# The query convolution of image 1 on TensorE, and a reordered lead-in, in a fused two-layer vision block

## The chip, the cores and the metric

The program runs on one core of one Trainium2 chip. The metric is the device time of one execution, in microseconds (us). Engines: TensorE (PE), VectorE (DVE), ScalarE (ACT), GpSimd (POOL), and SyncE (SP), whose queue issues most DMAs. Each engine runs its own list of instructions in order; semaphores make one engine wait for another. A change of 0.3% (4.8 us) is about what can be told from none.

## The reference, cut to what matters

The input is x, 4 images of 96 channels and 56 x 56 pixels, in f32. Two layers follow, each a token mixer and a mixture-of-experts FFN with a norm before each:

```
x = x + attention(norm_channels(x))        # layer 0
t = tokens(x);  t = t + moe(norm(t))       # 4 experts, top 2, 96 -> 384 -> 96, exact gelu
x = x + convs(norm_channels(x))            # layer 1: 7x7, 5x3, 3x5, separable 7 and 5
t = tokens(x);  t = t + moe(norm(t))

attention(x):                               # all convolutions depthwise 3x3
    value, query = dwconv(x, w_v), dwconv(x, w_q)             # stride 1
    key, off     = dwconv(x, w_k, 2), dwconv(x, w_off1, 2)    # stride 2, 28 x 28
    offset = gelu(layernorm(off)) @ w_off2
    grid   = tanh(offset + ref)                               # 784 sample points
    v      = bilinear samples of value at grid
    out    = (query^T key * scale) v  =  query^T (key v^T) * scale   # per head of 32 channels
    return w_out @ out
```

## The kernel before, in words

**Tiling.** A norm or FFN tile is 448 pixels (8 rows of the image), 7 tiles per image. For the attention an image is laid out as quarters: partition 4c+q holds channel c of a group of 32 channels and quarter q of the image, so there are 3 groups g of 128 partitions, each with 784 pixels of a quarter. A depthwise 3x3 tap is then one multiply by a number per partition.

**Order of work.** All engines walk the same list of steps, `STEPS`: a lead-in of 15 steps (slot -1, `LEAD = 15`), then 8 slots of 7 steps. A slot is the FFN of one image in one layer, a step one tile of it, and each step has 12 chunks `c` (4 experts x 3 blocks of 128 hidden units). In a chunk of an FFN step PE does the three products of `first` (L1206 to L1208, hi and lo parts of the weights and tokens), ACT the gelu (L1004), PE the product of `second` one chunk later (L1199), and DVE combines the experts (L1506). The lead-in has the same 12 chunks per step, but no FFN: it only prepares image 0 and 1 for slot 0. The order is written out by hand, in tables that say at which step and chunk which piece is issued.

**Norm tiles (jobs).** `START_JOBS` says which tile is normalized in which step of the lead-in: "a0" to "a2" are attention norms of image 0 to 2, "f0" the FFN norm of image 0. A step has a job at place 0 and one at place 1. A job is: PE turns the tile to tokens (L1151), DVE takes the statistics (L1478, L1482, L1489) and subtracts the mean (L1490), POOL takes the power -1/2 (L1049), ACT scales (`apply`, L869), PE turns it back (L1161), ACT moves it out (`move`, L888/L889), SP stores it to DRAM in `norm_a` (L628). A job of place 1 is turned back and moved in the next step. In the lead-in `apply` is at chunks 3 and 8, at chunk 8 for both jobs of step 7.

**Convolutions of attention.** `ON_PE` names which of them PE does (`tap_conv`, L1268): image 0's off, query (first half of the rows), key, query (second half), and image 1's off and key. Each is 9 products per group of channels, one per tap, added up in one PSUM bank (L1287). Each product is against a 128 x 128 block that holds the tap's weights on its diagonal. A query half is 392 columns for each product, a key or off 196. ACT takes each result out of the bank with the bias (`take_conv`, L902). There are two banks (`h_ps`), so a convolution waits until the one before the last has been taken. All other 3x3 convolutions run on DVE (`attn_taps`, `taps3`, L1547 for the first tap, L1550 for the other 8, 3 groups): value for each image, and in image 1 query too, spread over FFN steps 0, 1 and 2 of slot 0 (`Q_ROUNDS`).

**The diagonal blocks.** The off blocks are made by POOL in 7 operations (`DIAG_POOL`, L1056) at the end of lead steps 2 and 3, in the buffers gate_t, pair and hidden; the 27 query blocks by POOL in 3 operations at the end of lead step 4, in `res_mem`; the 27 key blocks by ACT in three sets of 9 (`make_key_diag`, L893), in step 5 at chunks 2, 5 and 8. `res_mem` later holds the residual of the image, so no query blocks are left for image 1.

**Taps.** 19 small DMAs bring the weights of all convolutions (9 for attention and `to_quarters` and 4 of layer 1 on ACT's queue ahead of any of its work, 6 on SP's). At the end of lead step 1 PE spreads them over the partitions (L1402), and ACT copies them to `all_w` (L1029). At the end of step 3 PE spreads w_out and then waits until DVE has made `w_exp` of it (L1441).

**Stages.** The attention of image 0 runs in stages 0 to 6 in lead steps 5 to 11, that of image 1 in stages 0 to 2 in lead steps 12 to 14 and stages 4 to 6 in FFN steps 0 to 2. Value is done in stages 0 and 1; in stage 2 PE turns its 7 blocks (L1217, chunks 3 to 9), ACT takes them (L914), SP stores them (`store_values`, L725) so that POOL can gather from them; DVE norms off, ACT does gelu (L936) and tanh (L940), DVE the positions (L1659 to L1674). POOL gathers the samples of 2 x 8 blocks (`gather`, L1076), and DVE weighs them (`sample_row`, L1696 to L1703). In stage 6 PE forms key v^T and its product with w_out (L1246, L1252) and multiplies the query with it in 8 pieces (`times_query`, L1264), which DVE adds to the residual (L1609).

**POOL's list** in lead steps 7 and 8: at the end of step 7 gathers 0 to 7 of image 0; in step 8 the power of the first job, gathers 8 to 15, the power of the second job. **SP's list** in stage 2: three value blocks' stores, the store of the step's first norm tile, then the other four blocks' stores.

**Between the lead-in and the FFN.** In lead step 14 DVE reads the first scores of the gates (L1718), ACT does their exp (L944, behind its table load), DVE ranks them (L1729 to L1753), PE turns them (L1321) at chunk 9 and goes on with scores at chunk 10. Before FFN step 0 PE waits until all the attention's convolutions have been taken (`cv_free`).

Of the kernel before, what the change touches and what calls it, by code (L numbers as in the profile page):

```python
# [20 lines left out]
E, HID = 4, 384  # L21
# [61 lines left out]
ON_PE = {0: ("off", "query", "key", "query"), 1: ("off", "key")}  # L83
# [65 lines left out]
def metaformer_kernel(nc, a, out):  # L149

    with ExitStack() as ctx:
# [165 lines left out]
        def in_blocks(*mems):  # L317
# [111 lines left out]
        A_PARTS = [("value",), ("value", "query")] + [("value", "off", "key", "query")] * (NB - 2)  # L429
# [10 lines left out]
        DIAG_RUNS = {"off": 7, "query": 10}  # L440
# [20 lines left out]
        QUERY_CONV = {(0, 9): (0, 0), (0, 10): (0, 1), (1, 3): (0, 2), (3, 2): (1, 0), (3, 8): (1, 1), (4, 2): (1, 2)}  # L461
        QUERY_TAKE = {(0, 11): (0, 0), (1, 2): (0, 1), (1, 5): (0, 2), (3, 8): (1, 0), (3, 11): (1, 1), (4, 5): (1, 2)}
# [1479 lines left out]
```

## Time and profile before

| | us |
|---|---|
| median of 3 runs | 1609.62 (1609.45 to 1614.06) |
| profiled execution: its own time | 1611.21 |
| span of the profile | 1609.4 |
| PE busy | 1431.7 (89%) |
| DVE busy | 1143.8 (71%) |
| ACT busy | 719.2 (45%) |
| POOL busy | 504.0 (31%) |
| mean granted clock of PE, of its full speed | 0.953 |

The profile is of one execution. An engine counts as busy while an instruction of its is running; the shares are averages over stages with different limits, so they do not say what sets the end. The first 223 us of the span are the lead-in, the next 92 us the first three FFN steps, in which the attention of image 1 runs too. An f32 product of PE leaves two records, so 9 products are 18 records.

### The profile page before, as it was taken

How to read it: one execution, taken by the hardware profiler on the slowest of the kernel's cores; microseconds unless marked ns; L12 is line 12 of the kernel's file. 1: busy time of each engine (PE TensorE's matmuls, PEld its weight loads, DVE VectorE, ACT ScalarE, POOL GpSimd, SP SyncE). 2: the span in 40 equal slices, each digit the busy share in tenths (PEclk: the TensorE clock that was granted, in tenths of full speed). 3: DMA queues.
4: the chain of work that ended last, by engine and by line, in shares of the span. 5: the costliest groups of instructions: out<-in, count | busy, mean ns of one | idle time of the engine just before them, and what ended most of it. 6: DMA issues, size and time to landing. Idle time of an engine off the chain costs nothing.

```text
span 1609.4 us, 21517 instructions
## 1 busy us (share of the span) xinstructions
PE 1431.7 (89%) x6736; PEld 1060.9 (66%) x6736; DVE 1143.8 (71%) x2881; ACT 719.2 (45%) x1481; POOL 504.0 (31%) x536
## 2 busy tenths in 40 slices
PE   5876758998869999998888999999999999998998
PEld 4654745555545677665555577787888788877786
DVE  6926878489984544359997444577787877689787
ACT  4432244246532344454553244454444544356554
POOL 5141032011350000011063000254344633465575
PEclk9987978999889999999989999999999999999999
DMA  5433035234333212441341422344234422221121
GB/s 121 103 92 104 20 99 131 58 96 119 91 78 93 82 56 52 107 121 56 100 127 49 134 65 61 76 111 103 66 78 111 114 66 60 72 77 60 56 69 56
DMA packets 168547, 136.37 MB, mean 85 GB/s; under 512 B 114928, under 2 KB 162162, under 8 KB 168050
## 3 DMA queue, kind: packets, MB, share of 16 engines
q1 hardware_dynamic: 163010, 129.71, 30.3%
q0 software_dynamic: 3072, 4.82, 1.3%
q8 instruction: 55, 0.90, 0.2%
q10 hardware_dynamic: 2352, 0.47, 0.2%
q14 instruction: 58, 0.48, 0.1%
HBM read 95.30 MB, written 39.13 MB: 84 GB/s over the span
## 4 chain that ended last, share of the span: by engine, by line
PE 49%; DVE 13%; issue 12%; POOL 6%; ACT 5%; SPq 1%; DMA 1%; ACTq 0%; POOLq 0%; DVEq 0%
PE at_ps L1345 9%; PE y_ps L1199 7%; PE h_ps L1206 5%; PE h_ps L1208 5%; PE h_ps L1207 5%; PE y_ps L1188 4%; POOL pix_mem L1076 3%; DVE vq_mem L1550 3%; PE y_ps L1189 3%; PE y_ps L1190 3%; PE at_ps L1264 3%; ACT ln_cen L869 2%; POOL ln_rstd L1049 2%; PE lb_ps L1161 2%; DVE part L1506 2%
## 5 line engine op out<-in xcount | busy, mean ns | idle before, releaser
L1004 ACT ACTIVATE hidden<-h_ps,b 128x448 f32<-128x448 f32 x609 | 384.7, 634 | 623.0 <-PE h_ps L1208 610.4
L1206 PE MATMUL h_ps<-xh,w1h 96*128 96x448 f32 x672 | 368.1, 548 | 2.5 <-ACT hidden L1004 1.3
L1049 POOL TENSOR_TENSOR ln_rstd<-ln_ve,minus_half 112x4 f32<-112x4 f32 x112 | 147.8, 1320 | 673.2 <-DVE ln_ve L1489 671.0
L1199 PE MATMUL y_ps<-hidden,w 128*96 128x448 f32 x672 | 326.0, 571 | 14.6 <-ACT hidden L1004 12.2
L1506 DVE SCALAR_TENSOR_TENSOR part<-y_ps,b,gate_t 96x448 f32<-96x448 f32 x224 | 151.3, 676 | 213.0 <-PE y_ps L1199 167.3
L1068 POOL CAST in_w<-hidden 128x448 fp32r<-128x448 f32 x273 | 198.7, 731 | 244.9 <-ACT hidden L1004 163.7
L1207 PE MATMUL h_ps<-xl,w1h 96*128 96x448 f32 x672 | 250.4, 373 | 0.0
L1208 PE MATMUL h_ps<-xh,w1l 96*128 96x448 f32 x672 | 249.6, 371 | 0.0
L1206 PEld LDWEIGHTS h_ps<-xh,w1h 96*128 96x128 f32 x672 | 130.5, 194 | 90.5 <-issue 60.8
L1207 PEld LDWEIGHTS h_ps<-xl,w1h 96*128 96x128 f32 x672 | 131.9, 196 | 67.6 <-issue 62.2
L869 ACT ACTIVATE ln_cen<-ln_cen,ln_rstd 112x96 f32<-112x96 f32 x448 | 130.2, 363 | 90.9 <-POOL ln_rstd L1049 90.8
L1550 DVE SCALAR_TENSOR_TENSOR vq_mem<-x_mem,all_w,vq_mem 128x770 f32<-128x770 f32 (+1 forms) x168 | 163.2, 1016 | 1.8 <-POOL ln_rstd L1049 0.7
L1432 DVE TENSOR_TENSOR in_w<-hidden,in_w 128x448 fp32r<-128x448 f32 x182 | 122.3, 679 | 55.1 <-POOL in_w L1068 54.9
L1199 PEld LDWEIGHTS y_ps<-hidden,w 128*96 128x96 f32 x672 | 104.2, 170 | 53.1 <-ACT hidden L1004 28.3
L1208 PEld LDWEIGHTS h_ps<-xh,w1l 96*128 96x128 f32 x672 | 129.8, 193 | 10.9
L1188 PE MATMUL y_ps<-in_w,w2h 128*96 128x448 f32 x273 | 116.3, 426 | 6.1 <-DVE in_w L1432 4.1
L1076 POOL DMA_INDIRECT pix_mem<-value_pairs,o_idx x64 | 91.0, 1422 | 55.4 <-DVE o_idx L1671 37.9
L1161 PE MATMUL lb_ps<-ident,ln_cen 112*96 112x112 f32 x448 | 69.2, 281 | 41.4 <-ACT ln_cen L869 32.6
L1478 DVE BATCH_NORM_STATS2 ln_stats<-lt_ps 112x6 f32<-112x96 f32 x412 | 77.0, 248 | 33.0 <-PE lt_ps L1151 33.0
L1189 PE MATMUL y_ps<-in_w,w2l 128*96 128x448 f32 x273 | 100.3, 367 | 0.0
L1161 PEld LDWEIGHTS lb_ps<-ident,ln_cen 112*96 112x96 f32 x448 | 48.6, 135 | 67.1 <-ACT ln_cen L869 59.7
L1345 PE MATMUL at_ps<-x_mem,kon_mem 120*84 120x224 f32 (+1 forms) x392 | 83.9, 346 | 0.0
(186 smaller groups left out, 2155.5 us busy)
## 6 DMA issues: line engine op xcount, KB each, us to landing
gate_t<-gates_dram SPq DMA_DIRECT2D x112, 336.0 KB, 3.2
value_pairs<-pix_mem SPq DMA_DIRECT2D x56, 168.0 KB, 3.2
x_mem<-norm_c SPq DMA_DIRECT2D x16, 420.0 KB, 4.4
res_mem<-in_x SPq DMA_DIRECT2D x4, 1176.0 KB, 11.1
x_attn<-res_mem SPq DMA_DIRECT2D x16, 294.0 KB, 2.7
res<-x_attn SPq DMA_DIRECT2D x28, 168.0 KB, 3.0
x_ffn<-ffn_out SPq DMA_DIRECT2D x28, 168.0 KB, 2.0
ln_x<-x_ffn SPq DMA_DIRECT2D x28, 168.0 KB, 3.2
```

Source lines behind the costliest of these rows:

```text
L869: ins = act.activation(ln_cen[n % CEN][:, s, :], ln_cen[n % CEN][:, s, :], ACT.Copy, scale=ln_rstd[n % 2][:, s:s + 1])
L1004: act.activation(to[:, :], h_ps[c % H_BANKS][:, 0:TILE], ACT.Gelu, bias=b1[l][:, c:c + 1]).then_inc(gelu_done, 1)
L1049: pool.tensor_tensor(ln_rstd[n % 2][:, :], ln_ve[n % 2][:, :], minus_half[0:SUB, 0:NSUB], ALU.pow)\
L1068: pool.tensor_copy(hi_ring[turn_of(u, c)], hid_ring[turn_of(u, c)][:, :]).then_inc(hi_made, 1)
L1188: pe.matmul(ps, w2h[:, c, :], hi, start=(j == 0), stop=False)
L1199: pe.matmul(y_ps[e % Y_BANKS][0:C, 0:TILE], w2[l][:, c, :], hidden[c % HID_RING][:, :], start=(j == 0), stop=(j == CPE - 1)).then_inc(hid_ ...
L1206: pe.matmul(ps, hi, xh[:, ring(k)], start=True, stop=False)
L1207: pe.matmul(ps, hi, xl[:, ring(k)], start=False, stop=False)
L1208: pe.matmul(ps, lo, xh[:, ring(k)], start=False, stop=True).then_inc(h_full, 1)
L1345: last = pe.matmul(ps[:, :, x0:x1], toep(g, dx), xt[:, :, g, x0 + dx - 3:x1 + dx - 3], start=(n % 7 == 0), stop=(n % 7 == 6))
L1506: dve.scalar_tensor_tensor(part[:, e, :], y_ps[e % Y_BANKS][0:C, 0:TILE], b2[l][:, e:e + 1], gate_t[e // 2][0:C, e % 2, :], ALU.add, ALU.m ...
L1550: ins = dve.scalar_tensor_tensor(dst, src, w, dst, ALU.mult, ALU.add)
```

## The change

The parts of the edit:

- **Query of image 1 on PE.** `ON_PE` gets two query halves for image 1; DVE's list for it has only value. `QUERY_CONV` and `QUERY_TAKE` place them: in stage 1 (lead step 13) at chunks 9 and 11, in stage 2 (lead step 14) at chunks 0, 1, 2 and 10.
- **Blocks.** ACT makes the query blocks of image 0 too (step 4 chunk 11, step 5 chunks 1 and 4), the key blocks move to step 6, chunks 0, 3 and 6, and ACT makes 27 blocks "query1" for image 1 in steps 12 and 13. They lie in part, hidden 0 and 3, res, ffn_out and to_quarters, which the FFN does not yet use (some grow to 128 partitions). POOL makes the off blocks alone, at the end of steps 3 and 4. The first load of `res` waits until the last convolution has run.
- **Start.** ACT's first table load stands ahead of its DMAs, and the 4 tap DMAs of layer 1 move from ACT's queue to SP's. Taps are spread at the end of step 2, not 1. PE's wait for `w_exp` moves to the first turn of off.
- **Jobs.** Step 7 has one norm tile, not two; the tiles behind it move by one place, and FFN steps 0, 1 and 2 take a2 4, 5 and 6 (before: step 0 a2 5 and step 2 a2 6).
- **Chunks.** In step 7 `apply` is at chunk 10 and turning back and `move` at chunk 11; in step 11 `apply` at chunk 7; gelu of image 0 at chunk 10, its tanh at 11.
- **Gathers of image 0** go in four groups of 4, with the powers of the norm tiles between them.

```diff
-              (-1, 7): [("a1", 4), ("a1", 5)], (-1, 8): [("a1", 6), ("a2", 0)], (-1, 9): [("a2", 1), ("a2", 2)],
-              (-1, 10): [None, ("a2", 3)], (-1, 11): [("a2", 4), ("f0", 0)], (-1, 12): [("f0", 1), ("f0", 2)],
-              (-1, 13): [("f0", 3), ("f0", 4)], (-1, 14): [("f0", 5), ("f0", 6)], (0, 0): [("a2", 5)],
+              (-1, 7): [("a1", 4)], (-1, 8): [("a1", 5), ("a1", 6)], (-1, 9): [("a2", 0), ("a2", 1)],
+              (-1, 10): [None, ("a2", 2)], (-1, 11): [("a2", 3), ("f0", 0)], (-1, 12): [("f0", 1), ("f0", 2)],
+              (-1, 13): [("f0", 3), ("f0", 4)], (-1, 14): [("f0", 5), ("f0", 6)], (0, 0): [("a2", 4)], (0, 1): [("a2", 5)],
-ON_PE = {0: ("off", "query", "key", "query"), 1: ("off", "key")}
+ON_PE = {0: ("off", "query", "key", "query"), 1: ("off", "key", "query", "query")}
...
+                "query1": in_blocks((part_mem[:, :, :].rearrange("p e n -> p (e n)"), 14), (hidden[0], 3), (hidden[3], 3),
+                                    (res_tile, 3), (out_tile, 3), (one_block, 1))}
...
-        A_PARTS = [("value",), ("value", "query")] + [("value", "off", "key", "query")] * (NB - 2)
+        A_PARTS = [("value",), ("value",)] + [("value", "off", "key", "query")] * (NB - 2)
...
+                      (0, 4, 2): (1, 2), (1, 1, 9): (0, 0), (1, 1, 11): (0, 1), (1, 2, 0): (0, 2), (1, 2, 1): (1, 0),
+                      (1, 2, 2): (1, 1), (1, 2, 10): (1, 2)}
+                      (0, 4, 5): (1, 2), (1, 1, 11): (0, 0), (1, 2, 0): (0, 1), (1, 2, 1): (0, 2), (1, 2, 2): (1, 0),
+                      (1, 2, 10): (1, 1), (1, 2, 11): (1, 2)}
-        DIAG_AT = {(5, 2): 0, (5, 5): 1, (5, 8): 2}
-        DIAG_POOL = {2: ((0, 7), (7, 9), (9, 14)), 3: ((14, 18), (18, 21), (21, 24), (24, 27)), 4: ((0, 9), (9, 18), (18, 27))}
+        DIAG_AT = {(4, 11): ("query", 0), (5, 1): ("query", 1), (5, 4): ("query", 2), (6, 0): ("key", 0),
+                   (6, 3): ("key", 1), (6, 6): ("key", 2), (12, 4): ("query1", 0), (12, 9): ("query1", 1),
+                   (13, 2): ("query1", 2)}
+        DIAG_POOL = {3: ((0, 7), (7, 9), (9, 14)), 4: ((14, 18), (18, 21), (21, 24), (24, 27))}
...
-                    for dst, src in tap_rows[4:]:
+                    for dst, src in tap_rows:
...
             def load_res(u, m):
                 sp.wait_ge(summed, 3 * (TILES * u + m))
+                if u == 0 and m == 0:
+                    sp.wait_ge(cv_full, CV_END[-1])
...
+            act.wait_ge(pool_set, 1)
+            act.activation(g_p[0][:, 0, 0:1], zeros[0:SUB, 0:1], ACT.Copy, scale=1.0)
             with nc.allow_non_contiguous_dma("small"):
...
-                for dst, src in tap_rows[:4]:
-                    load(dst, src)
-            act.wait_ge(pool_set, 1)
-            act.activation(g_p[0][:, 0, 0:1], zeros[0:SUB, 0:1], ACT.Copy, scale=1.0)
...
-            def make_key_diag(g):
+            def make_diag(name, g):
+                if name == "query1":
+                    act.wait_ge(w1_split, 2)
                 for t in range(9):
-                    ins = act.activation(diag["key"][9 * g + t], ident[:, :], ACT.Copy,
-                                         scale=w_a[:, TAPS_OF["key"], g, t:t + 1])
-                ins.then_inc(key_diag_set, 1)
+                    ins = act.activation(diag[name][9 * g + t], ident[:, :], ACT.Copy,
+                                         scale=w_a[:, TAPS_OF[name.rstrip("1")], g, t:t + 1])
+                ins.then_inc(diag_set, 1)
...
-                        if slot < 0 and c == (APPLY_DEEP[job.place] if deep(job) else LEAD_APPLY[job.place] if p != 7 else 8) or slot >= 0 and c == APPLY and job.place == 0:
+                        if slot < 0 and c == (APPLY_DEEP[job.place] if deep(job) else LEAD_APPLY[job.place] if p not in (7, 11) else 10 if p == 7 else 7) or slot >= 0 and c == APPLY and job.place == 0:
                             apply(job)
-                        if c == (MOVE if slot >= 0 else LEAD_MOVE) and job.place == 0 and not deep(job):
+                        if c == (MOVE if slot >= 0 else LEAD_MOVE if p != 7 else 11) and job.place == 0 and not deep(job):
...
-                if (slot, p) == (-1, 1):
+                if (slot, p) == (-1, 2):
                     act.wait_ge(taps_spread, 1)
...
                 if 3 in stages and stages[3] == 0:
-                    gather(0, 8, 2 * GQ)
+                    gather(0, 4, 8)
+                if 4 in stages and stages[4] == 0:
+                    gather(0, 12, 2 * GQ)
...
                 if 2 in stages and stages[2] in ON_PE:
-                    gather(stages[2], 0, 8 if stages[2] == 0 else 4)
+                    gather(stages[2], 0, 4)
+                if 3 in stages and stages[3] == 0:
+                    gather(0, 8, 12)
...
             def turn_off(b, h):
                 if h == 0:
+                    if b == 0:
+                        pe.wait_ge(wexp_done, 1)
```

## Rows read from the trace of the kernel before

**Rows 1.** The page, part 1: busy time, share of the span, instructions of each engine.

```profile
PE 1431.7 (89%) x6736; PEld 1060.9 (66%) x6736; DVE 1143.8 (71%) x2881; ACT 719.2 (45%) x1481; POOL 504.0 (31%) x536
```

**Rows 2.** Windows: stretch, length, busy us by engine, PE's granted clock, DMA share, GB/s.

```profile
189.00:223.20 34.20, 12.51 (x73) 10.93 (x71) 24.97 (x78) 16.34 (x33) 4.13 (x4) 0.63 0.32 77
...
223.20:251.70 28.50, 23.19 (x87) 15.36 (x88) 19.37 (x48) 13.49 (x25) 19.64 (x14) 0.85 0.29 81
251.70:273.50 21.80, 19.93 (x64) 12.37 (x62) 20.69 (x37) 7.75 (x13) 2.91 (x3) 0.84 0.76 180
273.50:314.70 41.20, 37.43 (x133) 20.81 (x131) 20.93 (x34) 9.98 (x19) 1.04 (x1) 1.00 0.19 56
```

**Rows 3.** Waits of PE, 199.2 to 314.7: line <- releaser: us, times, longest.

```profile
PE lg_ps L1174 <- DVE g_s L1718: 7.5, 1, 7.5
PE lg_ps L1321 <- DVE g_s L1753: 6.3, 1, 6.3
PE y_ps L1217 <- DVE vq_mem L1550: 5.0, 1, 5.0
PE lb_ps L1161 <- ACT ln_cen L869: 3.2, 1, 3.2
PE y_ps L1199 <- ACT hidden L1004: 2.1, 1, 2.1
...
PE y_ps L1199 <- DVE part L1506: 1.9, 1, 1.9
PE at_ps L1264 <- DVE vq_mem L1550: 1.0, 1, 1.0
```

**Rows 4.** Timeline of the opening: start, us, what, xcount, [idle before <- releaser].

```profile
9.98 2.21 ACT L869 ACTIVATE ln_cen<-ln_cen,ln_rstd 112x96 f32<-112x96 f32 x8
...
36.92 6.25 POOL L1056 TENSOR_TENSOR res_mem<-ident,all_w 128x1152 f32<-128x1152 f32 x3
...
37.42 4.82 PE L1287 MATMUL h_ps<-x_mem,gate_t 128*128 128x196 f32 x18 [1.66 <-issue]
```

**Rows 5.** Timeline of ACT and SP, 49 to 89, and the landing of pix_mem's DMAs.

```profile
49.79 2.74 ACT L893 ACTIVATE toep_own<-ident,all_w 128x128 f32<-128x128 f32 x9
...
84.14 1.28 ACT L936 ACT_TABLE_LOAD   x1
...
83.78 5.08 SPq L725 DMA_DIRECT2D value_pairs<-pix_mem  x8
...
DMA to landing us min/median/max: 2.5/2.8/3.6
```

**Rows 6.** Timeline of POOL's gathers and of PE behind them, 92 to 107.

```profile
93.12 1.19 POOL L1076 DMA_INDIRECT pix_mem<-value_pairs,o_idx  x1 [12.02 <-DVE o_idx L1671]
94.62 0.97 POOL L1076 DMA_INDIRECT pix_mem<-value_pairs,o_idx  x1 [0.30 <-issue]
...
105.88 0.88 PE L1217 MATMUL at_ps<-ident,kon_mem 128*98 128x128 f32 x3 [8.70 <-ACT kon_mem L902]
```

**Rows 7.** Timeline of PE: two query results of image 0, 9 products each.

```profile
62.81 6.02 PE L1287 MATMUL h_ps<-x_mem,res_mem 128*128 128x392 f32 x18
...
108.58 7.85 PE L1287 MATMUL h_ps<-x_mem,res_mem 128*128 128x392 f32 x18
```

**Rows 8.** Timeline of ACT and PE around the gates in lead step 14.

```profile
217.12 0.26 ACT L944 ACTIVATE g_p<-g_s 112x64 f32<-112x64 f32 x1
...
220.94 0.40 PE L1321 MATMUL lg_ps<-ident,g_s 112*64 112x112 f32 x1 [6.29 <-DVE g_s L1753]
```

**Rows 9.** DVE's query taps as a group, 223 to 290, and POOL beside them.

```profile
L1550 DVE SCALAR_TENSOR_TENSOR vq_mem<-x_mem,all_w,vq_mem 128x770 f32<-128x770 f32 (+1 forms) x24 | 23.1, 1015 | 0.0
...
233.04 4.55 POOL L1076 DMA_INDIRECT pix_mem<-value_pairs,o_idx  x1 [0.30 <-issue]
```

**Rows 10.** Timeline of PE: the first product of two chunks in a row.

```profile
262.20 0.72 PE L1206 MATMUL h_ps<-xh,w1h 96*128 96x448 f32 x1
...
263.56 0.71 PE L1206 MATMUL h_ps<-xh,w1h 96*128 96x448 f32 x1
```

More of the change, by code:

```diff
@@ L439, in metaformer_kernel @@
         CV_END = [sum(G * len(ON_PE[image]) for image in range(b + 1)) for b in ON_PE]
-        DIAG_RUNS = {"off": 7, "query": 10}
+        OFF_RUNS = 7
         AT_USES = 2 + VBLK + 2 + 1 + G + 2 * Q
@@ L963, in attention @@
                         take_off(b, ((0, 1), (8, 10))[b].index(c))
-                    if b == 0 and (stage, c) in QUERY_TAKE:
-                        take_conv(b, "query", *QUERY_TAKE[stage, c])
-                    if stage == 2 and c == 9:
+                    if (b, stage, c) in QUERY_TAKE:
+                        take_conv(b, "query", *QUERY_TAKE[b, stage, c])
+                    if stage == 2 and c == (10 if b == 0 else 9):
                         gelu_off(b)
@@ L969, in attention @@
                         take_conv(b, "key", 0, KEY_TAKE[b, stage, c])
-                    if stage == 2 and c == (10 if b == 0 else 11):
+                    if stage == 2 and c == 11:
                         tanh_pos(b)
@@ L1050, in scale_rows, with make_diags @@
                     .then_inc(ln_scale, 1)
-            def make_diags(name, first, last):
-                blocks = off_runs[first, last] if name == "off" else res_mem[:, 128 * first:]
+            def make_diags(first, last):
+                blocks = off_runs[first, last]
                 shape = [128, last - first, 128]
-                taps = w_a[:, TAPS_OF[name]].rearrange("p g t -> p (g t)")[:, first:last]
+                taps = w_a[:, TAPS_OF["off"]].rearrange("p g t -> p (g t)")[:, first:last]
                 pool.tensor_tensor(blocks[:, 0:128 * (last - first)].rearrange("p (t n) -> p t n", n=128),
@@ L1106, in _ @@
                 if slot < 0 and p in DIAG_POOL:
-                    if p == 2:
+                    if p == 3:
                         pool.wait_ge(ident_ld, 16)
@@ L1110, in _ @@
                     for first, last in DIAG_POOL[p]:
-                        make_diags("query" if p == 4 else "off", first, last)
+                        make_diags(first, last)
                 if 2 in stages and stages[2] in ON_PE:
-                    gather(stages[2], 0, 8 if stages[2] == 0 else 4)
+                    gather(stages[2], 0, 4)
+                if 3 in stages and stages[3] == 0:
+                    gather(0, 8, 12)
                 if 3 in stages and stages[3] not in ON_PE:
@@ L1269, in tap_conv @@
                 n = CV_AT[b, name][turn] + g
+                blocks = "query1" if (b, name) == (1, "query") else name
                 if n == CV_AT[b, "off"][0]:
@@ L1272, in tap_conv @@
                     pe.wait_ge(xq_direct, 16 * G * sum(image <= b for image in DIRECT))
-                if turn == 0 and name == "key":
-                    pe.wait_ge(key_diag_set, g + 1)
+                if turn == 0 and name == "off":
+                    pe.wait_ge(pool_diag_set, OFF_RUNS)
                 elif turn == 0:
-                    pe.wait_ge(pool_diag_set, DIAG_RUNS[name])
+                    pe.wait_ge(diag_set, G * ("query", "key", "query1").index(blocks) + g + 1)
                 if n >= H_BANKS:
@@ L1286, in tap_conv @@
                     c0, r0 = stride * x0 + dx - 1, turn * nr + dy
-                    last = pe.matmul(ps[:, :, x0:x1], diag[name][9 * g + dy * 3 + dx],
+                    last = pe.matmul(ps[:, :, x0:x1], diag[blocks][9 * g + dy * 3 + dx],
                                      rows[:, r0:r0 + stride * (nr - 1) + 1:stride, c0:c0 + stride * (x1 - x0 - 1) + 1:stride],
@@ L1297, in attention @@
                         turn_off(b, ((0, 1), (8, 10))[b].index(c))
-                    if b == 0 and (stage, c) in QUERY_CONV:
-                        tap_conv(b, "query", *QUERY_CONV[stage, c])
+                    if (b, stage, c) in QUERY_CONV:
+                        tap_conv(b, "query", *QUERY_CONV[b, stage, c])
                     if (b, stage, c) in KEY_CONV:
@@ L1372, in _ @@
                             turn_in(job)
-                        if c == (BACK if slot >= 0 else LEAD_BACK) and job.place == 0 and not deep(job):
+                        if c == (BACK if slot >= 0 else LEAD_BACK if p != 7 else 11) and job.place == 0 and not deep(job):
                             turn_back(job)
```

23 lines of the change are left out of this document (12 added, 11 removed).

## The prediction

> **What bounds the kernel now.** I read the page first: TensorE (PE) is busy 89% of the span of 1609.4 us [rows 1]. But that is an average over stages, so I read by stage, between events found in the timeline: the last key convolution of image 1 ends at about 189, FFN step 0 begins at 223.2, FFN step 3 begins at 314.7. The windows view gives these stretches [rows 2]. Before 223 PE is a third busy (12.5 of 34.2 us) at a mean clock of 0.63; in the first three FFN steps it is busy 23.2 of 28.5, 19.9 of 21.8 and 37.4 of 41.2 us, with the clock at 0.84 or 0.85 in the first two. So the lead-in is bound by chains through all engines, the FFN by PE with holes. The waits view names the holes [rows 3]: 5.0 us until VectorE (DVE) has the value convolution of image 1, 7.5 until it has read the scores, 6.3 until it has the gates; in the FFN steps 3.2 for a norm tile, 2.1 for a gelu behind ScalarE's (ACT) exp, 1.9 for DVE's combine, 1.0 for the query. After step 3 nothing changes but the order of a few norm tiles, so I count to the start of step 3 and carry the difference to the end.
>
> **1. Opening: -3.0 us.** ACT issues 13 small DMAs before it may apply the first norm at 9.98; DVE and GpSimd (POOL) had it ready 2 us earlier. After: table load first, nine DMAs, so about 7.8. Four DMAs go to SP's queue, ahead of w_out and the pad stores, some 2 us there, which the taps' move by a step covers. Then comes POOL: its query blocks (6.25 us from 36.92) go, and with them the time that a small operation of DVE stood beside them [rows 4]. But the offset blocks move a step later: 3.6 us of them now stand right before the first convolution. PE no longer waits for w_exp. I followed the norm tiles one by one with the durations of before (the first at ACT 2.2 us earlier; no stop for the taps' landing at the end of lead step 1, but the product of the taps at the end of step 2; no stop for w_exp, so that the tile that DVE begins at 32.8 begins at 26.5; then DVE, two powers and four block operations in a row on POOL): the last block is there at 34.3, and the first convolution at 34.4 instead of 37.42: -3.0. DVE's value convolution starts 9 us earlier, which PE hides, since it runs on its convolutions to 68.8, now 65.8.
>
> **2. Image 0's chain to its gathers: -6.6.** The three key block sets (9 blocks in 2.74 us each) move behind the query sets; the last stands in ACT's order behind the third query result (66.5), so ACT takes the value blocks from 69.25, about 1 us earlier than before. But no norm tile is applied between them any more (that cost ACT 7 us), so gelu's table load starts at 75.1, not 84.14: -9.0 [rows 5]. DVE's offsets, tanh and the positions follow as before, so the gathers could start at 84.3. But something new is late [rows 5]: eight of the 14 value stores (issued from 83.78 in 5.08 us) stand on SP behind the store of norm tile a1 4, whose move has gone to chunk 11 (78.2). 78.5 + 5.1 us of issue + 2.8 to land = 86.4, so the gathers start at 86.5, not 93.12.
>
> **3. Gathers in fours: -5 more at the first wait, at last -12.7.** Eight gathers of 1.27 us stand before a 1 us power on POOL, ACT stands behind that, and PE waits 8.70 us (the gathers start at 93.12, 1.27 us apart) [rows 6]. With four before it: 86.5 + 5.1 + 1.0 + ACT's apply and take 2 = 94.3 for PE instead of 105.88; PE then still stood 5 us, and its convolution stays at the low clock at its start. Its convolution begins 11.6 earlier (97.0 for 108.58 [rows 7]); PE's wait of about 1 us for ACT behind it goes: -12.7. All 16 gathers and the powers are still 22 us on POOL (to 112.7), ahead of DVE's sampling.
>
> **4. Lead steps 11 to 13: +1.4.** ACT copies m2 ahead of an apply: -0.5. In steps 12 and 13 it makes three more block sets, 8.2 us (three times 2.74); two lie in its idle time, but delay a move by 0.5, and the third stands before the take that frees PE's bank, 1.4: +1.9. With the -12.7 of part 3 this is -11.3: what PE did at 189.7, it does at 178.4.
>
> **5. The added convolutions: 54 products of 392 columns.** Nine of them (18 records) make one result. Image 0's are the same: nine ran in 6.02 us at 2.4 GHz, and in 7.85 when they began at 1.2 GHz behind PE's pause [rows 7]. Six are 36 us of PE, against 21 us of holes (34.2 - 12.5 is 21.7); and five stand before the value turns. In the time of before from 189.7: three of them with scores and a turn 18.0 + 1.1, the tile f0 5 in 0.35, the fourth 6.0, a turn back 0.4, the fifth 6.0: 221.4. DVE's value convolution (199.2) is no longer what is late. What is queued behind: the value turns, the last norm tiles, and behind them ACT's seven takes (4.8), its apply and take and exp (3.7, of which 1.28 table load), DVE's ranking 3.5 (from the exp's end at 217.38 to PE's turn at 220.94 [rows 8]), turn, takes and scores 3.1: 236.5. PE has stood since 227, so the sixth costs 7.9: 244.4, ACT's take 0.9: FFN at 245.3. Before 223.2: +22.1. Bounds: the holes filled perfectly give 36 - 21 = +15, the sixth wholly at 1.2 GHz (twice 6.0) gives +26. I take the worked order, nearer to the upper.
> The page "TensorE: Matmul & The Clock Gate" of the Trainium skill (Back-to-back issue gap) gives N/2.4 ns plus 2.5 warm and N/1.2 cold; the sixth would by it cost 6.0 or 11.8 us, and the sum move by -1.9 or +3.9 against the row's 7.9.
> With part 4 FFN step 0 begins at 178.4 + 55.6 = 234.0: +10.8.
>
> **6. FFN steps 0 to 2: -9.3.** DVE loses 24 operations of 1.015 us and three shorter ones: some 25 us [rows 9]. On PE this is worth only what waited for it. A chunk is 1.36 us (from 262.20 to 263.56 [rows 10]); 36 are 49, and transposes, keys, scores, the eight y products bring a floor of 74.5. Step 0: a gather beside the taps took 4.55 us, one without them 0.97 [rows 6, 9], so the power came late, and PE waited 3.2 and ran 4 us at half clock; both go, with the low clock at the start and ACT's wait for tanh there: 28.5 becomes 23.8. The exp wait 2.1 stays. Step 1: the 1.9 and its low clock go, tile a2 5 comes (about 1 us): 21.8 becomes 18.2. Step 2: 1.0 less: 40.2. Together 82.2 for 91.5 [rows 2, 3]. Bounds: the waits alone that name the taps, -2.9; the floor, -17. DVE is free, so I stay by the sum.
> Why the gather suffers, the page "SBUF — State Buffer" of the Trainium skill says (SBUF: two separate sides): a DVE operation with two SBUF inputs locks out GpSimd reads. By that rule, the trace agrees with 4.55 against 0.97 us.
>
> **Edits costed at nothing.** `res` is now loaded behind the last convolution; it is needed at the end of FFN step 0, some 20 us later, and SP then holds only the gate loads, which wait for the same event. POOL's powers between the gathers: DVE samples only after the last. The a2 tiles come a place later: image 2's taps wait for a2 6, which keeps its place in step 2. If that cover went, image 2's start would be late by a norm tile, about 3 us.
>
> **Sum:** -11.3 + 22.1 - 9.3 = +1.5 us. The profiled execution took 1611.21 around its span of 1609.4; the median of the runs is 1609.62, so I add to that: 1611.
>
> **Rivals.** *A, the FFN gets back more* (faster). PE, working through the lead-in's end, keeps 2.4 GHz: the sixth convolution at 6.0 (-1.9), no low clock behind the exp wait (-2.2), step 2's sum of y turns shorter as DVE is idle (-2), two starts in part 3 warm (-2), the value stores not last (-2): -10, 1601. For it: the mean clocks of 0.63 and 0.85 leave room. Against: the convolution behind the wait of 8.70 began at half clock [rows 6, 7].
> *B, the query on PE is dear* (slower). The lead-in's gain stands on one queue at four places (SP's stores, POOL's fours, ACT's block sets); if the chain of gathers gives half back (+6.3), or the FFN gains only the 2.9 us that name the taps (+6.4), the time is 1617 to 1618. It decides as soon as the lead-in's gain at the end of lead step 13 is below 8 us or the FFN's below 6. For it: of 25 us taken from DVE, PE's named waits show 2.9. Against: the 3.2 us wait is of the taps too, through POOL.
> *C, PE was never the matter before 223* (a variant of faster): the exp chain moves with DVE's normalise, not with PE, so the convolutions fall in the holes: +15 in place of +22, 1604. Against: the value turns stand on PE behind five of the six.
>
> **How the numbers follow.** This kernel can tell 0.3%, 4.8 us. Sum as worked: 0.42, its own range 1606 to 1616. A 0.17 and C 0.13, faster: 0.30. B 0.28, slower. The bounds taken one at a time give 1603 (-17 in the FFN), 1604 (+15 in the lead-in), 1615 (+26) and 1617.5 (-2.9); A reaches 1601 and B 1618, and I leave 3 us behind B and 1 behind A for their own error: 1600 to 1621 for 8 in 10. Faster 0.30, same 0.42, slower 0.28.
>
> **What would show it.** Part 1: the first L1287 at 34.4. Part 2: gelu's table load L936 near 75.1, the last L725 then the first gather near 86.5. Part 3: PE's wait before L1217 about 5 us, not 8.7. Part 5: 54 more products (108 records) of 392 and 385 columns in vq_mem's stead, value turns L1217 of image 1 near 210, 8 us after DVE's last value tap, first L1206 at 234. Part 6: no L1550 between 234 and step 3, that start at 316, the gathers all near 1.27 us apart. It is wrong if step 3 begins before 311 or after 320; a difference that first appears behind step 3 would be one that I have not seen.

## The result, and the profile after

The changed kernel takes 1618.64 us (median of 16 runs; the kernel before 1609.53, 16 runs): ratio 1.0048, 95% interval 1.0037 to 1.0059, or 6.0 to 9.5 us slower. The ratio is not the quotient of the two medians, which lie 9.1 us apart (the means 8.1). The time lies in the range given (1600 to 1621), but not within the 0.3% of "no change": 1611 was forecast, and the side of rival B came. The prediction also named a sign by which it would be wrong, step 3 beginning before 311 or after 320; it began at 324.3, so by its own sign the account is wrong, though the time is inside the range. The profiled execution took 1616.06 us around a span of 1614.2.

The page after, part 1 (busy time, share of the span, instructions), as in [rows 1]: PE has 108 records more and DVE 27 fewer, as foretold.

```profile
PE 1455.6 (90%) x6844; PEld 1072.8 (66%) x6844; DVE 1117.0 (69%) x2854; ACT 737.8 (46%) x1541; POOL 492.9 (31%) x533
```

The windows of the changed kernel that answer to [rows 2]: the lead-in from the event that stood at 189.20 before (it is the turn of image 1's offsets), then FFN steps 0, 1 and 2. Columns: stretch, length, busy us by engine, PE's granted clock (share of 2.4 GHz), DMA share, GB/s.

```profile
180.89:234.75 53.86, 44.93 (x178) 28.46 (x177) 26.09 (x80) 18.57 (x38) 3.65 (x3) 0.90 0.20 49
234.75:256.01 21.26, 19.06 (x87) 12.86 (x87) 7.00 (x32) 13.35 (x25) 10.91 (x11) 1.00 0.38 109
256.01:275.64 19.63, 19.21 (x71) 12.32 (x70) 12.17 (x35) 9.10 (x18) 8.01 (x7) 0.91 0.68 168
275.64:324.25 48.61, 39.98 (x133) 22.98 (x131) 17.32 (x30) 9.98 (x19) 1.05 (x1) 0.89 0.24 67
```

Read the lengths. At 180.9 the kernel is 8.3 us ahead. The added convolutions turn that into +11.6 at FFN step 0 (234.75 for 223.18). Steps 0 and 1 are 7.3 and 2.2 us shorter than before, but step 2 is 7.4 longer (48.6 for 41.2), so step 3 begins 9.6 us late (324.25 for 314.70). The waits of PE in these three steps name what is new (line <- releaser: us, times, longest); all the waits of [rows 3] that came from DVE's taps are gone:

```profile
PE at_ps L1263 <- DVE kon_mem L1717: 5.9, 1, 5.9
PE at_ps L1281 <- DVE res_mem L1627: 2.6, 4, 0.7
PE y_ps L1214 <- ACT hidden L1016: 2.1, 1, 2.1
PE h_ps L1221 <- issue: 0.7, 1, 0.7
PE lb_ps L1176 <- ACT ln_cen L879: 0.4, 1, 0.4
```

L1263 is image 1's keys times sampled values. Its chain goes back through DVE's samples to the gathers on POOL (timeline: start, us, what, [idle before <- releaser]):

```profile
249.81 0.97 POOL L1088 DMA_INDIRECT pix_mem<-value_pairs,o_idx  x1 [0.30 <-issue]
264.35 1.05 POOL L1061 TENSOR_TENSOR ln_rstd<-ln_ve,minus_half 112x4 f32<-112x4 f32 x1 [13.57 <-DVE ln_ve L1507]
265.63 1.47 POOL L1088 DMA_INDIRECT pix_mem<-value_pairs,o_idx  x1 [0.23 <-issue]
...
280.44 0.96 DVE L1714 TENSOR_TENSOR kon_mem<-pix_mem,o_cw 98x768 f32<-98x768 f32 x1 [7.27 <-DMA pix_mem<-value_pairs,o_idx]
...
285.00 2.93 PE L1263 MATMUL at_ps<-kon_mem 98*128 98x128 f32 x12 [5.91 <-DVE kon_mem L1717]
```

POOL had sent off ten of the 16 gathers by 250.8. Then it stood 13.6 us at the power of norm tile a2 5, which the change had moved into FFN step 1; the last six gathers are queued behind it. Before, step 1 had no norm tile, and they ran on, from 247.41 to 255.3. The same 12 records of PE that took 1.60 us at 277.04 before then take 2.93, at a granted clock of 0.50.

Behind step 3 the two kernels do the same work. This pair of executions ends only 4.8 us apart. In one stretch alone it lost 3.0 us of the 9.6: the kernel before ran from 518 to 544 at a granted clock of 0.87, and the changed one did the same 104 records at 1.00 in 23.0 us (526.4 to 549.4). Why the clocks differed there is open. The medians carry the difference, not this pair.

### The profile page after: what moved, and what is told of

The parts are those of the page before. It is cut to its first block, busy times and chain, and to the rows that moved or that the text cites. A ratio compares the mean times of both kernels' runs of the same rounds, so it can differ in the third digit from the quotient of the medians.

```text
span 1614.2 us, 21770 instructions
## 1 busy us (share of the span) xinstructions
PE 1455.6 (90%) x6844; PEld 1072.8 (66%) x6844; DVE 1117.0 (69%) x2854; ACT 737.8 (46%) x1541; POOL 492.9 (31%) x533
## 4 chain that ended last, share of the span: by engine, by line
PE 50%; issue 12%; DVE 11%; POOL 7%; ACT 5%; DMA 1%; SPq 0%; ACTq 0%; POOLq 0%; DVEq 0%
PE at_ps L1363 10%; PE y_ps L1214 7%; PE h_ps L1221 5%; PE h_ps L1223 5%; PE h_ps L1222 5%; POOL pix_mem L1088 4%; PE y_ps L1203 3%; PE y_ps L1204 3%; PE y_ps L1205 3%; PE at_ps L1281 3%; DVE vq_mem L1568 2%; ACT ln_cen L879 2%; POOL ln_rstd L1061 2%; PE lb_ps L1176 2%; PE lg_ps L1189 1%
## 5 line engine op out<-in xcount | busy, mean ns | idle before, releaser
L1221 PE MATMUL h_ps<-xh,w1h 96*128 96x448 f32 x672 | 364.1, 542 | 3.3 <-ACT hidden L1016 1.3
L1061 POOL TENSOR_TENSOR ln_rstd<-ln_ve,minus_half 112x4 f32<-112x4 f32 x112 | 143.9, 1285 | 678.0 <-DVE ln_ve L1507 677.8
L1214 PE MATMUL y_ps<-hidden,w 128*96 128x448 f32 x672 | 321.9, 564 | 14.0 <-ACT hidden L1016 13.4
L1568 DVE SCALAR_TENSOR_TENSOR vq_mem<-x_mem,all_w,vq_mem 128x770 f32<-128x770 f32 (+1 forms) x144 | 140.1, 1016 | 1.8 <-POOL ln_rstd L1061 0.7
L1496 DVE BATCH_NORM_STATS2 ln_stats<-lt_ps 112x6 f32<-112x96 f32 x412 | 77.1, 248 | 34.4 <-PE lt_ps L1166 34.4
L1176 PEld LDWEIGHTS lb_ps<-ident,ln_cen 112*96 112x96 f32 x448 | 48.3, 134 | 56.3 <-ACT ln_cen L879 47.1
```

The costliest lines, as they stand in the source:

```text
L1061: pool.tensor_tensor(ln_rstd[n % 2][:, :], ln_ve[n % 2][:, :], minus_half[0:SUB, 0:NSUB], ALU.pow)\
L1214: pe.matmul(y_ps[e % Y_BANKS][0:C, 0:TILE], w2[l][:, c, :], hidden[c % HID_RING][:, :], start=(j == 0), stop=(j == CPE - 1)).then_inc(hid_ ...
L1221: pe.matmul(ps, hi, xh[:, ring(k)], start=True, stop=False)
L1568: ins = dve.scalar_tensor_tensor(dst, src, w, dst, ALU.mult, ALU.add)
```

## The experiments

Times are medians; "ratio" is against the kernel before, run beside them. "FFN 0" and "step 3" are the starts of FFN steps 0 and 3 in the profiled execution. The starts of the lead-in differ by 1 to 2 us from one execution to the next, so these columns are good to that. The medians are of 5 to 16 runs, the kernel before itself had medians of 1609.5 to 1611.2 beside them, and a difference of two medians is good to some 2 to 3 us: by the means of the same runs, e1, e4 and e5 lie 6.9, 3.1 and 3.4 us under the changed kernel, not 8.4, 4.0 and 5.1. Where a size matters, the trace is read beside it.

| kernel | us | ratio (95%) | first conv. | FFN 0 | steps 0-2 | step 3 |
|---|---|---|---|---|---|---|
| before | 1609.5 | 1 | 37.4 | 223.2 | 91.5 | 314.7 |
| changed | 1618.6 | 1.0048 (1.0037-1.0059) | 38.6 | 234.8 | 89.5 | 324.3 |
| e1 gathers first | 1610.3 | 1.0009 (0.9997-1.0022) | 38.5 | 237.0 | 80.6 | 317.6 |
| e2 sixth early | 1619.8 | 1.0060 (1.0042-1.0078) | 39.4 | 233.1 | 94.4 | 327.5 |
| e3 query on DVE | 1608.9 | 0.9995 (0.9985-1.0005) | 39.7 | 214.6 | 97.5 | 312.1 |
| e4 w_out early | 1614.7 | 1.0028 (1.0015-1.0041) | 33.9 | 231.6 | 89.9 | 321.5 |
| e5 stores first | 1613.5 | 1.0018 (1.0002-1.0034) | 38.5 | 230.2 | 89.5 | 319.7 |
| e6 sixth behind turns | 1614.2 | 1.0025 (1.0010-1.0039) | 39.1 | 227.7 | 91.8 | 319.4 |
| e7 lead-in alone | 1603.1 | 0.9948 (0.9930-0.9966) | 38.7 | 213.3 | 92.1 | 305.4 |
| e8 query placed | 1601.4 | 0.9946 (0.9928-0.9964) | 38.6 | 228.4 | 80.1 | 308.5 |
| c1 repairs, query on PE | 1592.3 | 0.9882 (0.9860-0.9904) | 33.0 | 216.8 | 80.1 | 296.9 |
| c2 repairs, query on DVE | 1593.8 | 0.9882 (0.9858-0.9905) | 34.1 | 205.3 | 94.4 | 299.7 |
| e9 one product | 1581.6 | 0.9815 (0.9792-0.9839) | 34.1 | 205.3 | 82.2 | 287.5 |
| c3 per group | 1590.3 | 0.9869 (0.9848-0.9890) | 32.4 | 215.1 | 80.1 | 295.2 |

**e1: the six gathers ahead of the power.**

```diff
-                if 0 in jobs:
+                if 0 in jobs and (slot, p) != (0, 1):
                     scale_rows(jobs[0])
...
                     gather(stages[5], 14, 2 * GQ)
+                if 0 in jobs and (slot, p) == (0, 1):
+                    scale_rows(jobs[0])
```

> Edit: in FFN step 1 GpSimd issues the last six gathers of image 1 first and takes the power of norm tile a2 5 behind them. Theory Q (one queue place): in the changed kernel these six gathers stood from 251 to 265.6 behind that power, which waits for DVE's statistics of a tile that PE turns in step 1; so the samples were late, and PE waited 5.91 us for them at the keys times values and then ran 2.9 us of products at half clock. Then the sixth-last gather follows at 251.1, the last ends near 258.5, PE's wait at L1263 is gone, step 2 falls from 48.6 to about 41.5 us, and the time from 1618.6 to 1611.5 (1610 to 1613). Rival F (PE is full with the added convolutions, the wait only shows where the load appears): another wait takes its place, step 2 stays above 46 us, time 1616 to 1619.

Measured 1610.25: 8.4 us less, by one place in a queue (steps 0 to 2 take 8.9 us less in the traces, 80.6 for 89.5). Windows of FFN steps 0 to 2, and POOL's last gather with the power behind it:

```profile
237.01:258.27 21.26, 19.07 (x86) 12.87 (x87) 7.00 (x32) 13.36 (x25) 14.80 (x15) 1.00 0.42 120
258.27:277.94 19.67, 19.25 (x72) 12.27 (x70) 14.58 (x38) 9.10 (x18) 2.99 (x3) 0.91 0.72 174
277.94:317.59 39.65, 36.94 (x133) 20.86 (x131) 14.85 (x28) 9.99 (x19) 1.01 (x1) 1.00 0.25 73
```

```profile
259.71 0.97 POOL L1088 DMA_INDIRECT pix_mem<-value_pairs,o_idx  x1 [0.30 <-issue]
266.62 1.05 POOL L1061 TENSOR_TENSOR ln_rstd<-ln_ve,minus_half 112x4 f32<-112x4 f32 x1 [5.95 <-DVE ln_ve L1509]
```

Step 2 is 39.65 at full clock (48.61 at 0.89), and no wait at L1263's place is left. Theory Q holds, rival F falls.

**e2 and e6: the sixth convolution ahead of the gates.**

```diff
-                      (1, 2, 2): (1, 1), (1, 2, 10): (1, 2)}
+                      (1, 2, 2): (1, 1), (1, 2, 8): (1, 2)}
```

> Edit: the sixth query convolution of image 1 stands on PE ahead of the turn of the gates (chunk 8 of lead step 14) instead of behind it. Its bank is free (the fourth result was taken at 207.5). Theory Q: it fills the hole of 7.79 us in which PE waits for the gates (216.4 to 224.1), at 6.0 us and full clock; FFN step 0 then begins at 227 instead of 234.75, tanh no longer stands behind the take of the sixth result, and the gathers of image 1 start 6 us sooner (231). The wait for the samples in step 2 stays (the power of a2 5 moves with PE's steps): 1611 (1610 to 1613). Rival F: exp, gates and the last norm tile are delayed by as much as PE is now occupied, FFN step 0 begins after 232, time 1616 to 1619.

Measured 1619.75: nothing gained. The theory's number was missed by nearly 9 us, and what rival F foretold came (FFN step 0 after 232). Chunk 8 lies ahead of the last two value turns. PE and ACT of e2:

```profile
223.31 0.81 PE L1305 MATMUL h_ps<-x_mem,one_block 128*128 128x385 f32 x2
223.96 0.82 PE L1232 MATMUL y_ps<-ident,vq_mem 128*112 128x128 f32 x6
224.49 0.81 ACT L926 COPY pix_mem<-y_ps 112x384 f32<-112x384 f32 x1 [3.50 <-PE y_ps L1232]
225.31 1.28 ACT L956 ACT_TABLE_LOAD   x1
226.61 0.26 ACT L956 ACTIVATE g_p<-g_s 112x64 f32<-112x64 f32 x1
...
230.42 0.39 PE L1339 MATMUL lg_ps<-ident,g_s 112*64 112x112 f32 x1 [5.64 <-DVE g_s L1771]
```

The convolution ends at 223.96, then come the two turns, their takes, and behind these ACT's exp. So the convolution held up the very chain that the hole waits for. Counted from the first value turn (212.33 and 214.99, since e2's execution was already 2.7 us later there), the gates come 3.6 us later than in the changed kernel and FFN step 0 only 4.4 us sooner. FFN step 0 then starts at half clock (granted 0.50, 0.57 us for a product that takes 0.36), the wait for the samples is 7.0, and steps 0 to 2 take 94.4 for 89.5: the 4.4 are gone. In e6 the convolution stands one turn further:

```diff
                     turn_value(b, c - TURNS)
+                if (b, stage, c) == (1, 2, 9):
+                    tap_conv(b, "query", 1, 2)
```

> Edit: the sixth query convolution stands on PE behind the last value turn and ahead of the turn of the gates. In e2 it stood ahead of the last two value turns by mistake; ACT's last two takes and its exp queue behind these, so the exp came at 226.61 instead of 220.33 and PE waited 5.6 us again. Theory Q: behind the turns it delays nothing; the hole of 7.79 falls below 2 us, FFN step 0 begins 6 to 8 us sooner relative to the last key convolution (at 227 for 234.75), tanh is no longer behind the sixth result, and the last gathers still wait for the power of a2 5: 1611.5 (1610 to 1613). Rival F: 1616 to 1619, FFN step 0 after 232.

Measured 1614.19: 4.5 us less, outside the theory's range (1610 to 1613) and below the rival's. The wait for the gates fell from 7.79 to 1.94, and FFN step 0 began at 227.65. But the last six gathers still stood behind the power, and in step 2 the wait at the keys times values grew from 5.91 to 6.86; step 0 ran at a clock of 0.87 and took 24.1 us, not 21.3.

**e3: the query back on DVE.**

```diff
-ON_PE = {0: ("off", "query", "key", "query"), 1: ("off", "key", "query", "query")}
+ON_PE = {0: ("off", "query", "key", "query"), 1: ("off", "key")}
...
-        A_PARTS = [("value",), ("value",)] + [("value", "off", "key", "query")] * (NB - 2)
+        A_PARTS = [("value",), ("value", "query")] + [("value", "off", "key", "query")] * (NB - 2)
```

(and the entries of image 1's query in the three tables of places)

> Edit: the query convolution of image 1 is back on DVE (27 taps beside FFN steps 0 to 2), all else of the change stays, with the norm tile in FFN step 1. Theory Q (the moved lead-in is worth what it showed, 8.3 us at 181, the added convolutions cost +20 before FFN step 0 and give back little): FFN step 0 begins near 214 (223.2 less 9, since DVE ends the value taps 9 us sooner), FFN steps 0 to 2 take 91.5 us as before plus 2 to 7 for the gathers behind the tile's power: step 3 at 308 to 313, time 1603 to 1608. Rival: the lead-in's gain is lost anyway at the gates or at the gathers beside the taps, step 3 at 314 or later, time 1609 or more.

Measured 1608.88, just outside the theory's range: FFN step 0 at 214.55 as expected, but steps 0 to 2 took 97.5, with 5.68 us of wait for the samples. The gathers' place costs this version 5.8 us too (e7 below), so e3 alone says little of the convolutions.

**e4: the copy of w_out in DVE's idle time.**

```diff
+                if (slot, p) == (-1, 2):
+                    expand_w_out()
                 if (slot, p) == (-1, 3):
-                    expand_w_out()
+                    set_w_exp()
```

(`set_w_exp` is the part of `expand_w_out` from its wait for `wexp_ps` on)

> Edit: DVE's copy of w_out into quarters (4.37 us in the changed kernel, beside GpSimd's first block operations; 1.00 us before) stands one lead step earlier, in DVE's idle time at 16.2; the products and w_exp stay. Theory C (DVE and GpSimd slow each other down, and PE stood 5.5 us for the copy): the copy takes about 1 us, the first block operations less than 3.47, PE's wait of 5.54 at 27.58 goes, the first offset convolution starts near 34.5 instead of 38.63, and 3 to 4 us of it arrive at FFN step 0: 1615 (1614 to 1616.5). Rival: GpSimd's block operations of lead step 4 follow the norm tiles' powers and remain last, or the gain is absorbed by the chain of the gathers: first convolution within 1 us of 38.6, or time 1617.5 to 1619.

Measured 1614.65, 4.0 us less. The opening of the changed kernel first, then that of e4:

```profile
23.16 4.37 DVE L1454 COPY hidden<-w_out 96x384 f32<-96x384 f32 x1
23.84 3.47 POOL L1068 TENSOR_TENSOR gate_t<-ident,all_w 128x896 f32<-128x896 f32 x3
...
27.58 1.59 PE L1148 MATMUL at_ps<-ident,hidden 96*128 96x96 f32 x6 [5.54 <-DVE hidden L1454]
...
38.63 1.62 PE L1305 MATMUL h_ps<-x_mem,gate_t 128*128 128x196 f32 x4 [4.88 <-POOL hidden L1068]
```

```profile
16.14 0.35 DVE L1454 COPY hidden<-w_out 96x384 f32<-96x384 f32 x1
22.10 1.46 PE L1148 MATMUL at_ps<-ident,hidden 96*128 96x96 f32 x6
24.11 3.47 POOL L1068 TENSOR_TENSOR gate_t<-ident,all_w 128x896 f32<-128x896 f32 x3
...
33.94 5.54 PE L1305 MATMUL h_ps<-x_mem,gate_t 128*128 128x196 f32 x18 [4.87 <-POOL hidden L1068]
```

The copy falls from 4.37 to 0.35 us and the first convolution comes at 33.94 (34.4 had been predicted for the change). POOL's blocks take 3.47 in both. One half of the expectation was wrong: POOL was not slowed, DVE alone was. The copy ended at 27.53, 0.2 us behind POOL's third operation at 27.31.

**e5: the value stores ahead of the norm store on SP.**

```diff
-                if 0 in jobs:
+                if 0 in jobs and (slot, p) != (-1, 7):
                     store_norm(jobs[0])
...
                         store_values(stages[2], j)
+                if (slot, p) == (-1, 7):
+                    store_norm(jobs[0])
```

> Edit: on SP's queue the store of norm tile a1 4 (lead step 7) stands behind all 14 value stores of image 0 instead of behind the sixth. Theory S (the last value store's landing starts the gathers): in the changed kernel eight value stores left SP from 82.5 to 87.4, and the gathers began at 90.95 though the indices were ready at 87.9. With the stores issued as ACT takes the blocks, they are out near 80, the gathers start at 88 to 88.5, and 2.5 to 3 us of it come through to FFN step 0: 1616 (1615 to 1617). Rival: the DMA of the gathers waits for something else (PE's wait before the value turns of the offsets grows by the same amount), or the later store of a1 4 delays its quarter load: 1618 to 1620.

Measured 1613.51: 5.1 us less (3.4 by the means), against 2.5 to 3 expected. The gathers began at 89.02 (90.95), 1.9 us sooner. In the traces more is added behind PE's wait for them, where the clocks differ; the changed kernel first, then e5:

```profile
98.62 0.88 PE L1232 MATMUL at_ps<-ident,kon_mem 128*98 128x128 f32 x3 [4.50 <-ACT kon_mem L914]
...
101.32 6.93 PE L1305 MATMUL h_ps<-x_mem,res_mem 128*128 128x392 f32 x18
```

```profile
96.67 0.53 PE L1234 MATMUL at_ps<-ident,kon_mem 128*98 128x128 f32 x3 [2.56 <-ACT kon_mem L916]
...
98.09 6.03 PE L1307 MATMUL h_ps<-x_mem,res_mem 128*128 128x392 f32 x18
```

Behind a wait of 2.56 PE's transposes took 0.53 us for three and the convolution 6.03, at a granted clock of 1.00; behind 4.50 they took 0.88 and 6.93, with a mean of 0.75 over both. So PE was 1.95 us sooner at the end of the wait, 3.2 at the convolution and 4.1 at its next wait (115.41 for 119.48). The other runs agree: the transposes took 0.53 or 0.54 in the five runs whose wait there was 2.56 or less, and 0.88 in all with 4.49 or more.

**e7 and e8: query on DVE against query on PE, both with e1's repair.** e7 is e3 with e1's edit. e8 is the changed kernel with e1's edit, and the fifth and sixth convolutions both where e6 has the sixth.

> The moved lead-in with the query convolution of image 1 on DVE (as in e3) and the six gathers ahead of the power of a2 5 (as in e1); nothing else. e3 measured 1608.9 with a wait of 5.7 for the samples in FFN step 2. Theory Q: that wait falls to 1 or 2 (c2 showed 1.36), so 1604 (1602 to 1606): this is what the lead-in alone is worth without the queue place. Rival: DVE's taps slow the gathers that now run beside them, 1607 or more.

> The changed kernel with two queue places repaired: the gathers ahead of the power of a2 5, and the fifth and sixth query convolutions between the last value turn and the turn of the gates. The opening and the value stores stay as in the changed kernel, so e7 against e8 is the query on DVE against the query on PE. Theory Q: e1 measured 1610.3; the value turns come 6 us sooner, the hole of 7.8 is filled: -8 to -9: 1601.5 (1599 to 1604), level with or up to 3 us below e7. Rival (c1 gained by the repaired lead-in, not by the place of the two convolutions): above 1605 and above e7.

Measured 1603.08 and 1601.35, both within their ranges; their ratios (0.9948 and 0.9946) can't be told apart. e8 begins FFN step 0 15 us later and is through steps 0 to 2 12 us sooner.

**c1 and c2: all repairs.** c1 is e8 with the edits of e4 and e5; c2 is e7 with the same two.

> All repairs together, query of image 1 on PE: gathers ahead of the power of a2 5, w_out's copy early, value stores ahead of the norm store, and the fifth and sixth query convolutions both between the last value turn and the turn of the gates. Theory Q: -7.5 (e1 measured -8.4), -3.5 (e4 measured -4.0), -2.5, and the value turns 6 us sooner with both convolutions in the hole, -9: 1618.6 - 22.5 = 1596 (1593 to 1600). Rival: the repairs overlap (each ends at the next queue), 1602 to 1606.

> The same repairs with the query convolution of image 1 on DVE, as in the kernel before (no added convolutions). From e3 (1608.9; FFN step 0 at 214.55, steps 0 to 2 in 97.5 us with a wait of 5.7 for the samples): -6 for the gathers, -3.5 and -2.5 in the lead-in: 1597 (1595 to 1600). If this is below c1, the query convolution on PE is a loss by itself; theory Q says they are within 3 us of each other, since PE wins in FFN steps 0 to 2 (80.6 against 91.5 us) what it pays before them. Rival: DVE's 24 taps keep the gathers slow beside them (4.6 us each) and the repair of their order gives only 2 to 3: 1600 to 1603.

Measured 1592.30 and 1593.79, by the ratio both 1.2% under the kernel before; the two can't be told apart either. Both lie just below their ranges, 3 to 4 us under the forecast; 2 to 3 of that is e5, which had been put at 2.5. Within the noise the repairs add up: 8.4 (e1), 4.0 (e4), 5.1 (e5) and the 8.9 from e1 to e8 are 26.4, and c1 is 26.3 under the changed kernel. That the two agree to 0.1 is luck, since each term is good to 2 or 3 us; by the means they are 22.2 and 24.8. Windows of c1 from the third offset convolution of image 1 on, then FFN steps 0 to 2:

```profile
157.00:216.79 59.79, 57.34 (x264) 41.26 (x265) 39.19 (x110) 21.81 (x48) 5.66 (x5) 1.00 0.18 44
216.79:238.05 21.26, 19.06 (x86) 12.88 (x87) 7.00 (x32) 13.35 (x25) 14.78 (x15) 1.00 0.46 120
238.05:257.25 19.20, 17.81 (x71) 11.20 (x70) 14.58 (x38) 9.09 (x18) 2.98 (x3) 1.00 0.73 171
257.25:296.87 39.62, 36.92 (x132) 20.89 (x131) 14.82 (x28) 9.97 (x19) 1.01 (x1) 1.00 0.28 77
```

PE is busy 57.3 of the 59.8 us ahead of FFN step 0 and has full clock throughout. Most of c2's waits of PE from 168 to 300 are holes that c1 fills (in c1 the longest wait of this stretch is 2.1):

```profile
PE lg_ps L1190 <- DVE g_s L1739: 7.5, 1, 7.5
PE lg_ps L1340 <- DVE g_s L1774: 6.3, 1, 6.3
PE lb_ps L1177 <- ACT ln_cen L878: 5.7, 2, 3.2
PE y_ps L1233 <- DVE vq_mem L1571: 5.0, 1, 5.0
...
PE lg_ps L1190 <- ACT ln_cm L898: 2.5, 1, 2.5
```

**e9: what 54 products cost where c1 has them.**

```diff
+                    if blocks == "query1" and i > 0:
+                        break
```

> Kernel c1 with eight of the nine products of each of image 1's six query convolutions left out (48 products; the query of image 1 is then not computed in full). It asks what the 54 products cost PE where they now stand: 48 of 54 are 32 us of PE's work. Theory H (two thirds of it lies in holes that c2 shows: FFN step 0 at 205.3 there, 216.8 in c1): FFN step 0 begins near 205, steps 0 to 2 take 80 as in c1, so 1592.3 - 11.5 = 1581 (1579 to 1584). Rival (PE's order is already bound by it in full): 1570 or below; rival (exp, gates and the value turns are the bound in c1, not PE): 1588 or above.

Measured 1581.55, as theory H had it: 48 products of some 0.66 us, 32 us of PE's work, are worth 10.8 us; two thirds lie in holes. The kernel leaves out most of image 1's query, so it is a measure of cost and not a faster kernel. The holes come back at once (window ahead of FFN step 0: PE's busy time is 30.0 of 48.3 us, its clock 0.83):

```profile
157.00:205.30 48.30, 30.02 (x168) 26.39 (x169) 37.69 (x109) 22.56 (x49) 5.71 (x5) 0.83 0.22 55
```

**c3: the first convolutions wait for their own blocks.**

```diff
-                    pe.wait_ge(pool_diag_set, OFF_RUNS)
+                    pe.wait_ge(pool_diag_set, (2, 4, OFF_RUNS)[g])
```

> Kernel c1, and each of the three offset convolutions of image 0 waits only for the block operations that make its own nine blocks (two, four, seven of GpSimd's operations) instead of all seven. In c1 PE waited 4.87 us for the last of them, and the first convolution began at 32.98. Now the first needs operations done at 26.6, and waits for the last load of the input instead (issued 27.8 to 29.7, some 2 us to land): it begins at 31 to 32, and the three end 1 to 2 us sooner. Theory: the chain of image 0 starts at PE's convolutions, so 1 to 2 us come through: 1590.8 (1589.5 to 1592). Rival: DVE's value taps or ACT's key blocks are last there, no change: 1592 to 1593.

Measured 1590.32, the fastest that computes everything, 1.3% under the kernel before. Its 2 us over c1 are as expected, but the two intervals overlap, so they are not shown. The first convolution began at 32.42 (32.98), no longer behind POOL.

## Why the prediction missed, step by step

**Step 1, the opening (-3.0, measured +1.2): wrong.** The norm tiles were followed with the durations of before, in which the copy of w_out took 1.00 us. The edit moved POOL's first blocks beside it. e4 shows the price: 4.7 us at the first convolution, 4.0 in the end. The trace of before had the sign of it: a DVE operation with so few elements that it takes 0.17 us elsewhere took 2.98 us from 22.19, beside POOL's same three operations (21.67, 3.47 us), and ended with them. The prediction had seen such a row, for the query blocks (the same small operation took 5.77 us from 37.44), and counted what their going gives back; it did not ask what the offset blocks would hold up at their new place. The rows of before (timeline of POOL and DVE):

```profile
21.67 3.47 POOL L1056 TENSOR_TENSOR gate_t<-ident,all_w 128x896 f32<-128x896 f32 x3
22.19 2.98 DVE L1489 TENSOR_SCALAR ln_ve<-ln_mv 112x4 f32<-112x4 f32 x1
...
37.44 5.77 DVE L1489 TENSOR_SCALAR ln_ve<-ln_mv 112x4 f32<-112x4 f32 x1
```

The page "SBUF — State Buffer" of the Trainium skill (SBUF: two separate sides) calls the pair of ports that DVE and GpSimd share an exclusive lock, held for a whole instruction, while the other engine is blocked. The traces agree in that the copy stood (4.37 us beside POOL, 0.35 alone), but it stood for longer than one instruction: it ended behind the last of three.

**Step 2, the chain to the gathers (-6.6, measured -2.2): the mechanism was right, the size inherited the opening.** gelu's table load came at 79.01 (75.1 predicted, 84.14 before), then the stores behind the norm store held the gathers, as said. e4 and e5 each give a part back (gathers at 87.43 and 89.02 for 90.95; 86.5 had been predicted).

**Step 3, fours (first wait 5 us, then -12.7): measured 4.50, and -9.4.** The gain over step 2, 7.2 us, is near the 6.1 foretold.

**Step 4 (+1.4): measured +1.1** (-9.4 became -8.3; PE's new wait for ACT's third block set is 0.93 us at 166.66).

**Step 5, the convolutions (+22.1, measured +19.9): right in kind.** PE waited 7.79 us for the gates with the sixth behind them, as described; the sixth then took 7.5 us. The prediction took that order as given; from e1 to e8 another order is worth 8.9 us. That FFN step 0 began at 234.75, where 234.0 was forecast, is luck: steps 1 to 4 came 3.0 us short, and this one cost 2.2 less.

**Step 6, FFN steps 0 to 2 (-9.3, measured -2.0): this is the step that made the forecast wrong, by 7.3 of the 8.1 us at step 3.** Its sum was good: without the queue place e1 measures -10.9 (80.6 for 91.5), and step by step 21.3, 19.7 and 39.7 where 23.8, 18.2 and 40.2 were predicted. What failed is the paragraph "Edits costed at nothing": of the a2 tiles that come a place later it named who reads them, not what is queued behind them. One power on POOL, waiting for a tile of FFN step 1, had six gathers behind it; 8.4 us of median (e1).

**The rivals.** B's numbers came nearly (1617 to 1618; the FFN's gain was under 6), but not its reason: the taps were worth more than the 2.9 us that named them, and what ate them was a place in a queue. A's warm starts are real in part (FFN step 0 at clock 1.00, but the sixth convolution took 7.5 us and not 6.0) and were swamped. C is refuted by FFN step 0 at +11.6; in c1 the convolutions do lie mostly in holes (e9), with the last two behind the value turns.

So the lead-in alone, without the queue place, is worth 0.5% (e7), and the query convolution on PE is worth nothing measurable either way (e7 against e8, c1 against c2). A split of the query between PE's holes and DVE was not tried.

## What to carry to other kernels

A step that moves to an empty slot is not free there: list, for each engine that it touches, what is queued behind its first wait, and follow that to its reader. Work put into an engine's hole helps only if it stands behind everything that feeds the chain which the hole waits for (e2 against e6). And when an edit brings two engines' operations side by side that were apart, take their durations from a row in which they stood side by side.

## What was not expected of the hardware

- A DVE copy of 96x384 took 0.35 us alone, 1.00 in the kernel before (beside a GpSimd power), and 4.37 when it began 0.7 us ahead of the record of three GpSimd multiplications (3.47 us) that followed a GpSimd power without a gap. It ended 0.2 us behind the last of them; GpSimd's own time did not change.
- Two waits of PE in the same place, 2.56 and 4.50 us, left its granted clock at different levels (1.00, and 0.75 on average over the next 9.2 us): the next convolution of nine products took 6.03 and 6.93 us.
- In the changed kernel, without DVE's taps beside them, 14 of image 1's 16 gathers took 0.97 or 1.05 us; the two that met DVE's samples (265.2 to 268.2) took 1.47 and 1.61. In e7, with the taps back on DVE, one took 4.75.
